# Two MLP blocks and one VectorE step are moved, and GpSimd waits once more at the start, in a fused attention and MLP layer

## What is computed

```python
def attn_ref(x, ln1_g, ln1_b, wq, wk, wv, wo, ln2_g, ln2_b, w1, w2):
    x = x + _linear_attention(_layernorm(x, ln1_g, ln1_b), wq, wk, wv, wo)   # elu+1 features, 16 heads
    h = _layernorm(x, ln2_g, ln2_b)
    return x + _lookup_act(h @ w1) @ w2       # FF = 1024, gelu of a grid of steps of 0.1
def ffn_ref(x, CB, SCB, bias):
    return jnp.einsum('bsk,nk->bsn', x, CB) * (SCB * (1.0 / 127.0)) + bias
x = x + attn_ref(_layernorm(x), ...)
x = x + ffn_ref(_layernorm(x), CB, SCB, bias)
```

## Time and profile before

| | us |
|---|---|
| median of 3 runs | 592.0 |
| the profiled execution's own time | 592.04 |
| its span | 590.3 |
| busy: TensorE matmuls | 548.4 (93%) |
| busy: VectorE | 467.0 (79%) |
| busy: ScalarE | 389.7 (66%) |
| busy: GpSimd | 339.7 (58%) |

### The profile page before, as it was taken

One profiled execution on the slowest core, in us unless ns is written; L12 is line 12 of the kernel. 1 busy time (PEld: TensorE's weight loads), 2 busy tenths in 40 slices (PEclk: granted clock), 3 DMA queues, 4 the chain that ended last, 5 costly groups with the idle time before them and its releaser, 6 DMA issues.

```text
span 590.3 us, 11273 instructions
## 1 busy us (share of the span) xinstructions
PE 548.4 (93%) x3610; PEld 490.7 (83%) x3610; DVE 467.0 (79%) x1067; ACT 389.7 (66%) x636; POOL 339.7 (58%) x328
## 2 busy tenths in 40 slices
PE   7799999999998989999999999999999999999895
PEld 6678788888887879889898898988989888898785
DVE  5889999598776687878879788797887978879635
ACT  1475664456566776867768677686776867767670
POOL 3531333315132467686776867768677776777654
PEclk9799998899999999999999999999999999999999
DMA  8321221112011010110101011010110101100001
GB/s 273 120 72 46 97 71 37 36 37 72 2 37 57 0 37 1 71 41 30 72 0 71 36 37 72 0 71 36 36 71 0 71 36 36 71 0 36 37 1 74
DMA packets 11419, 29.47 MB, mean 50 GB/s; under 512 B 2048, under 2 KB 4864, under 8 KB 11392
## 3 DMA queue, kind: packets, MB, share of 16 engines
q1 hardware_dynamic: 9472, 28.32, 13.2%
q10 hardware_dynamic: 1920, 0.79, 0.6%
HBM read 20.71 MB, written 8.39 MB: 49 GB/s over the span
## 4 chain that ended last, share of the span: by engine, by line
PE 57%; DVE 23%; issue 8%; ACT 7%; POOL 3%; DMA 1%; DVEq 0%; ACTq 0%; POOLq 0%; SPq 0%
PE psum L1012 52%; PE psum L1030 4%; DVE bn_stats_b L664 4%; DVE f32r_arena L817 4%; DVE f_arena L854 3%; POOL f32r_arena L378 2%; DVE bn_stats L664 2%; ACT f_arena L486 2%; DVE mean_var L671 1%; DVE f32r_arena L703 1%; DVE n_and_ones L691 1%; ACT psum L509 1%; ACT f_arena L508 1%; DVE f_arena L710 1%; ACT f_arena L517 1%
## 5 line engine op out<-in xcount | busy, mean ns | idle before, releaser
L1012 PE MATMUL psum<-w_hi,f32r_arena 128*128 128x256 f32 x1280 | 176.2, 283 | 16.6 <-DVE f32r_arena L809 13.0
L1012 PEld LDWEIGHTS psum<-w_hi,f32r_arena 128*128 128x128 f32 x1280 | 163.5, 188 | 30.8 <-DVE f32r_arena L809 16.1
L1012 PE MATMUL psum<-f32r_arena,w_hi 128*128 128x512 f32 x512 | 141.1, 402 | 0.9 <-issue 0.9
L378 POOL TENSOR_TENSOR f32r_arena<-f_arena,f32r_arena 128x512 fp32r<-128x512 f32 x64 | 83.4, 1304 | 90.3 <-ACT f32r_arena L594 68.0
L581 ACT ACTIVATE grid_index<-psum,w_bias_in_steps 128x512 int8<-128x512 f32 x128 | 87.3, 682 | 56.4 <-PE psum L1012 56.4
L1012 PEld LDWEIGHTS psum<-f32r_arena,w_hi 128*128 128x128 f32 x512 | 88.1, 188 | 14.4 <-issue 1.1
L592 ACT ACTIVATE f_arena<-grid_index 128x512 f32<-128x512 int8 x128 | 80.9, 632 | 23.4 <-POOL f32r_arena L378 14.2
L594 ACT ACTIVATE f32r_arena<-grid_index 128x512 fp32r<-128x512 int8 x128 | 79.1, 618 | 0.0
L1012 PE MATMUL psum<-f32r_arena 128*128 128x256 f32 (+1 forms) x384 | 71.6, 336 | 2.4 <-DVE f32r_arena L703 2.4
L809 DVE TENSOR_TENSOR f32r_arena<-f_arena,f32r_arena 128x512 fp32r<-128x512 f32 x64 | 67.1, 1050 | 3.0 <-ACT f32r_arena L594 3.0
L1012 PEld LDWEIGHTS psum<-f32r_arena 128*128 128x128 f32 x384 | 59.2, 195 | 8.8 <-issue 2.6
(11 more groups left out here) (116 smaller groups left out, 917.8 us busy)
## 6 DMA issues: line engine op xcount, KB each, us to landing
f_arena<-in_L_attn_x_dram SPq DMA_DIRECT2D x32, 512.0 KB, 3.3
out_dram<-f_arena SPq DMA_DIRECT2D x15, 512.0 KB, 2.7
f_arena<-in_L_attn_w_dram SPq DMA_DIRECT2D x2, 1024.0 KB, 12.0
out_dram<-f_arena SPq DMA_DIRECT2D x2, 256.0 KB, 2.2
phi_q<-in_L_attn_wk_dram ACTq DMA_DIRECT2D x1, 256.0 KB, 4.8
phi_q<-in_L_attn_wq_dram SPq DMA_DIRECT2D x1, 256.0 KB, 5.1
phi_q<-in_L_ffn_CB_dram SPq DMA_DIRECT2D x1, 256.0 KB, 7.2
phi_q<-in_L_attn_wo_dram SPq DMA_DIRECT2D x1, 256.0 KB, 7.5
```

The lines of the kernel that those rows point to most:

```text
L378: nc.gpsimd.tensor_tensor(t_lo[m % SLOTS], tf[m % 2], t_hi[m % SLOTS].bitcast(F32), ALU.subtract).then_inc(s["t_lo_p"], 1)
L1012: return nc.tensor.matmul(out_, lhs, rhs, start=start, stop=stop, skip_group_check=True)
```

## The change

In TensorE's body `up(i, 1)` leaves the head of the body; `up(i+1, 1)` now comes right behind `up(i+1, 0)`, ahead of `down(i, 7)`. In VectorE's body `mlp_low(i, 0)` goes to the front, ahead of xp, and the two statistics steps of xp go behind `attn_low(i+1)`. GpSimd waits for `n1_ready` before it makes wk's low half.

```diff
             g.wait_ge(s["wk_hi_done"], 1)
+            g.wait_ge(s["n1_ready"], 1)
             nc.gpsimd.tensor_tensor(wk_lo, wk_raw, wk_hi.bitcast(F32), ALU.subtract).then_inc(s["wk_lo_done"], 1)
...
             def body(i, prv, main, nxt, nn):
+                if main:
+                    mlp_low(i, 0)
                 if prv:
                     c = i - 1
                     v.wait_ge(s["w2_tile"], c * MT + (MT + SLOTS))
                     v.wait_ge(s["xz_ready"], c + 1)
                     v.wait_ge(s["xb_ready"], i + 1)
                     ve.tensor_tensor(xp, two(BB), xz, ALU.add).then_inc(s["xp_ready"], 1)
-                    v.wait_ge(s["xp_ready"], c + 1)
-                    sums(xp, bn_b, "bn3")
-                    mean_var(i - 1, bn_b, mv3, "bn3", "mv3_ready")
-                if main:
-                    mlp_low(i, 0)
                 if is_chunk(i, 0):
                     attend(1, 1)
                     mlp_low(i, 1)
                 if nxt:
                     attn_low(i + 1)
+                if prv:
+                    v.wait_ge(s["xp_ready"], c + 1)
+                    sums(xp, bn_b, "bn3")
+                    mean_var(i - 1, bn_b, mv3, "bn3", "mv3_ready")
...
                 def body(i, prv, main, nxt, attend_seq, attended):
-                    if main:
-                        up(i, 1)
                     if is_chunk(i, 0):
...
                     if nxt:
                         up(i + 1, 0)
+                        up(i + 1, 1)
                     down(i, 7)
 
                 up(0, 0)
+                up(0, 1)
                 body(0, False, True, True, 0, 0)
```

## The result

The changed kernel takes 611.41 us (median of 4 runs, 608.42 to 611.59). The kernel before takes 591.51 us, now with a fourth run (590.93 to 592.23). The ratio is 1.0324, 95% interval [1.0289, 1.0359]: slower by 3.2%. The profiled execution took 611.4 us. The prediction was 610.7, from 601 to 617.

What follows compares the result with a forecast made beforehand. Two things were taken to hold a chunk: VectorE's work ahead of down 0 and, half a microsecond behind, ahead of down 3. Sum: 592.04 + 18.3 (chunks) + 1.2 (last chunk) - 0.8 (start) = 610.7 us, range 601 to 617.

Steps and rivals of the forecast that it cites:

- The chunk, 1.31 us: Chunks 1 to 14: down 3 starts 15.95 us behind up 0 instead of 14.64, 1.31 us longer each, 18.3 in all.
- TensorE's stands: In a chunk TensorE waits before down 1 (a few tenths), the residual's rows (0.7), down 2 (0.6), down 3 (1.0 us).
- The power comes into the way: GpSimd's power, hidden before, comes late behind xp's later statistics; VectorE stands about 1.2 us before the normalise.
- The hold on block 3's low half: VectorE's block 3 low half meets GpSimd's long L396 and ends 0.55 us behind it, at 397.82 us.
- first rival: Block 3's low half isn't held by GpSimd: 0.74 us a chunk, 602.8 us in all; 10%.
- The moves on TensorE: nothing by themselves: On TensorE up 1 and down 7 change places; the same matmuls run, so no cost by itself.
- The last chunk, 1.2 us: Last chunk: VectorE's low halves held by L413 and L386, the normalise later; +1.2 us, ends 0 and 1.6.
- The start, -0.8: Program start: GpSimd's wait keeps L324 out of VectorE's L681; -0.8 us taken, ends 0 and -0.94.
- rival 2: L413 on GpSimd also holds VectorE's first L809 and delays xp: 0.6 us a chunk more, 619.1 us; 8%.
- Rival 3: TensorE's two idle pieces in the loop vanish and nothing replaces them: 1.05 us a chunk won, 576.5 us; 8%.

Runs made afterwards that it cites:

- e6: The changed kernel with block 3's low half ahead of the first residual in VectorE's queue: 599.9 us, ratio 1.0159 to the kernel before.
- e8: e7 with block 3's low half moved between the first residual and its statistics: 584.24 us, ratio 0.9899 to the kernel before.
- e5: The changed kernel without up 1's move on TensorE: 609.26 us, ratio 1.0312 to the kernel before.
- e2: The kernel before with only up 1 moved ahead of down 7: 602.83, 605.75, 615.85 and 612.81 us, ratio 1.0336.
- e1: The kernel before with only GpSimd's new wait for n1_ready at the start: 590.27 us, ratio 1.0017.
- e3: The kernel before with only block 0's low half moved in front of xp: 597.38 us, ratio 1.0135.
- e4: The kernel before with xp's statistics moved behind the attention rows, so block 0's low half stands right behind xp: 605.55 us, ratio 1.0288.
- e7: The kernel before with GpSimd's wait at the start and block 0's low half between xp and its statistics: 582.0 us, ratio 0.9854.
- e10: e8 with GpSimd's bias sum cut into four pieces of 128x256: 580.33 us, ratio 0.9838 to the kernel before.
- e9: The changed kernel with GpSimd's bias sum cut into four pieces of 128x256: 606.66 us, ratio 1.0272 to the kernel before.

## Why the prediction was right

Laid over the spans, the 19.3 us come from four stretches: the start of up 0 of the first loop chunk, 14 chunks, the last one up to its last VectorE instruction, and what follows.

| | before | after | difference | predicted |
|---|---|---|---|---|
| to up 0 of the first chunk | 208.27 | 205.88 | -2.39 | -0.8 |
| 14 chunks | 345.41 | 363.60 | +18.19 | +18.3 |
| last chunk, from up 0 | 33.88 | 35.31 | +1.43 | +1.2 |
| to the end | 2.74 | 4.81 | +2.07 | 0 |

**The chunk, 1.31 us: right, step by step.** Counted from up 0, with the prediction's time in brackets: block 0's L810 3.21 us (3.23), xp 3.82 (3.83), attention rows 4.96 (5.09), block 1 8.12 (8.27), power 8.92 (9.08), normalise 10.05 (10.16), first residual 11.35 (11.54), GpSimd's sum 12.86 (12.97), down 3 15.85 (15.95). The chain is 0.12 us shorter than foreseen between xp and the attention rows, and stays 0.1 to 0.2 ahead from there: L818 follows xp by 1.14 us here (392.32 to 393.46), where I had taken the 1.26 to L664 in the earlier trace rows, an instruction that first waits for xp's result. From down 3 to the next up 0 TensorE takes 10.27 us and not 10.16, which gives the 0.1 back. So the 1.30 us a chunk that the up 0's show (18.19 / 14) rest on two errors of 0.1 us that cancel.

**TensorE's stands: the right four, the last three too large.** Foreseen: a few tenths, 0.7, 0.6, 1.0. Measured: 0.20, 0.59, 0.38, 0.70. (As said above, down 3 is late by more than its bracket, 0.86 us.)

**The power comes into the way: right.** The normalise stands 1.27 us for it; 1.2 was foreseen. Counted from up 0 the normalise starts at 10.05 us where it was 8.43, and 1.27 of these 1.62 us are the wait for the power. e6 points the same way: it still has this wait and is still 0.67 us a chunk slower than before, but its VectorE also runs in the new order. A kernel in which only the power is faster was not tried, so the power's share of the loss is argued and not shown.

**The hold on block 3's low half: right.** L397 ends at 403.75 and L810 at 404.29, 0.54 us behind, against 0.55 taken from before. The Trainium skill (SBUF — State Buffer, section "SBUF: two separate sides") has it that the engine that starts first keeps the port pair for its whole instruction and the other is blocked meanwhile. e8 agrees more sharply than the kernel before could show: a start 0.10 us ahead, and at 460 us one 0.02 us ahead, decides between 0.68 and over 2.8 us. The first rival (not held, 602.8) falls with the row of 1.33.

**"The moves on TensorE: nothing by themselves": right only inside this change.** e5 shows it there. The sentence is false of the move alone, which e2 has at +0.98 a chunk. It holds because block 0's low half, not down 7, decides when xp may start.

**The last chunk, 1.2 us: +1.43.** VectorE, its end:

```profile
572.52 1.70 DVE L810 TENSOR_TENSOR f32r_arena<-f_arena,f32r_arena 128x512 fp32r<-128x512 f32 x1 [3.47 <-ACT f32r_arena L595]
...
577.24 1.11 DVE L810 TENSOR_TENSOR f32r_arena<-f_arena,f32r_arena 128x512 fp32r<-128x512 f32 x1
579.61 1.38 DVE L801 TENSOR_SCALAR f_arena<-f_arena,mean_var,rstd 128x256 f32<-128x256 f32 x4 [1.27 <-POOL rstd L360]
```

The first L810 meets GpSimd's L414, the second L387, and the normalise waits 1.27 us for the power, where the earlier trace rows had 0.99. These are the three steps foreseen. Not foreseen was what TensorE does beside them: it stands 0.90 us before down 0 and 1.88 before down 1, and from 580 to 582 us its granted clock is 0.50, the lower level. It seems to have cost nothing, since from the normalise to the last VectorE instruction it is 25.18 us now and 25.23 before.

**The start, -0.8: the step that failed.** The hold was taken away as foreseen, but e1, with nothing but the wait, isn't faster. I had costed what follows as a chain that moves along, and the sum left out what the next chunk's statistics would then wait for: the transfer of x, which the earlier trace rows could not show because it came just in time (19.71 us, no wait). The lower end that the prediction gave this term, 0, was the right one. The -2.39 us of the table is no gain of this change either. The profile of e1 has -2.88 there, and its time is not shorter; e3, without the wait, also reaches its first xp earlier, at 210.17 us against 210.92 before. The stretch varies from one execution to the next, and one source of that is plain in the rows. TensorE's granted clock near 100 us (by stretches of 4 us, columns as in e2), before:

```profile
100.00:104.00 4.00, 4.00 (x17) 3.81 (x18) 2.75 (x3) 0.18 (x1) 3.88 (x4) 0.50 0.01 4
104.00:108.00 4.00, 4.00 (x10) 3.15 (x10) 0.93 (x3) 0.00 (x0) 2.79 (x5) 0.50 0.00 0
```

and in e1:

```profile
100.00:104.00 4.00, 4.00 (x15) 3.34 (x15) 2.45 (x3) 0.18 (x1) 3.91 (x5) 0.61 0.00 0
104.00:108.00 4.00, 4.00 (x20) 3.37 (x20) 1.21 (x5) 0.26 (x1) 2.51 (x4) 0.97 0.02 4
```

The low clock lasts over two such stretches in one execution and about one in the other, in the same program at this place. It shows in the time only where it lasts that long: in the kernel before, VectorE's normalise at 109.50 us stood 1.32 us for TensorE, and from one chunk's statistics to the next (96.80 to 110.80 us) it took 14.00 us, where the other twelve profiles have 12.58 to 12.61. So 1.4 of the 2.39 us are the slow stretch of that one profile. The other 1.0 was there already where the fourth chunk's statistics start, at 28.85 us before and 27.85 in the changed kernel. It is not the wait's either: e1, with the wait, has 28.59 there, and e2 to e4, without it, 28.32 to 28.61.

**The end.** +2.07 us lies behind the last VectorE instruction, where the last store goes out. Its two transfers of 256 KB land after 2.2 us before and 3.2 after, which is half of it; the other half I did not follow. They take 3.2 in e1, 3.0 in e5, 2.9 in e7 and 2.1 in e10, and the whole stretch is 4.65, 4.34, 4.20 and 2.56 us there, in faster and slower kernels alike. So it is scatter, like the first row, and the two nearly cancel. The forecast's 610.7 against the profiled 611.4 looks better than its parts: the chunk term was right to 0.1 us in 18, while start and end missed by 1.6 and 2.1 us with opposite signs.

**The others.** L413 (now L414) holds nothing: it ends at 391.43 us, before the first L810 at 391.71; rival 2 was ruled out by 0.28 us. Rival 3's idea, that the two old stands on TensorE might vanish and nothing take their place, did not come true for this change, but most of it can be had: e7 has one stand of 0.62 us, before the attention rows' product, in place of the two of 0.85 and 0.20, and e7 and e10 take 24.1 us a chunk in place of 24.75.

## What to carry to other kernels

- In a strictly ordered queue, count for each step moved forward what is pushed back behind it, and follow that to the far end of every round trip. Here 1.86 us of statistics moved back, and the round trip through GpSimd that they start came out of hiding.
- A short instruction on VectorE that has to be done soon belongs just ahead of the event that releases a long one on GpSimd, not just behind it; or cut the long one in pieces where the order of the two can't be made safe.
- Before a gain at the start of a program is counted, follow it to the next transfer that the engine waits for.

## What the runs showed of the hardware beyond what I expected

- The hold between VectorE and GpSimd goes both ways, and is decided by hundredths of a microsecond: L810 0.68 us and the sum 2.94, or L810 2.84 and the sum 2.39 (e8). In one profile both outcomes occur without any change of the program, at 1.3 us a chunk.
- Four 128x256 sums on GpSimd took 2.82 us where no L811 ran into them and 3.27 where one did (e9); one sum of 128x1024 took 2.39 to 2.41.
- One stand of 1.75 us on TensorE was followed by the lower clock and cost 1.3 us (e2); stands of the same 1.75 us in e3 (before the x16 at 240.02 and 265.24 us) left the granted clock at 1.00. In the last chunk a stand of 1.88 us was followed by the lower clock in the changed kernel, e3, e5 and e9 and not in e6, and one of 2.51 us in e2 (before 571.98 us) left it at 1.00. Four stands in one chunk, the longest 0.70 us, left it at full speed in the changed kernel's loop. So the length of one stand does not tell which it will be.
- The low-clock stretch near 100 us begins in or right behind 32 matmuls of one column each, before which TensorE stood 0.71 us, and lasts a different time in each execution. The 32 took 5.76 us before, 4.95 in the changed kernel and 3.73 in e1. It made the stretch up to 110 us 1.4 us longer in one of 13 profiles and in no other.
